# A graph layer with decaying weights: eight beats to a difference in three unmarked pairs, and their products four slots later

## The reference

```python
h = relu(layernorm(x))
support = h @ weight
mask = (adj != 0)
rank = cumsum(mask, axis=1)
deg = rank[:, -1:]
k = minimum(deg, 100)
pos = rank - (deg - k)
w = mask * where(pos > 0, 0.5 ** (k - pos), 0)
out = x + w @ support + bias
```

## Time and profile before

| what | us |
|---|---|
| median of 3 runs (216.24 to 216.45) | 216.44 |
| the profiled execution | 216.8 |
| its span in the trace | 214.2 |
| PE busy | 196.7 (92%) |
| DVE busy | 196.8 (92%) |
| ACT busy | 160.6 (75%) |

### The profile page before, as it was taken

The page is one execution under the profiler, slowest core; times in us unless marked ns, Lnnn a source line. Parts: engine busy times, 40 slices in busy tenths (PEclk is TensorE's granted clock), DMA queues, the critical chain, the costliest instruction groups (busy, mean ns, idle before and its releaser), DMA issues.

```text
span 214.2 us, 6505 instructions
## 1 busy us (share of the span) xinstructions
PE 196.7 (92%) x2784; PEld 188.0 (88%) x2784; DVE 196.8 (92%) x239; ACT 160.6 (75%) x303; POOL 29.1 (14%) x53
## 2 busy tenths in 40 slices
PE   0369979999999999999999999999999999999993
PEld 0269657997898999999999999999999999999993
DVE  1999979797979999999999999989999999998893
ACT  2442996786786988778778778789978989998720
POOL 7800000000010404010004110500000000000000
PEclk9999999999999999999999999999999999999999
DMA  6999999999999999999999999999998000000001
GB/s 203 204 217 220 216 211 216 216 219 212 218 213 221 210 218 216 213 220 216 211 222 212 217 218 215 216 217 218 221 209 174 8 12 3 12 15 3 17 0 43
DMA packets 7677, 36.09 MB, mean 168 GB/s; under 512 B 1506, under 2 KB 3298, under 8 KB 3554
## 3 DMA queue, kind: packets, MB, share of 16 engines
q0 software_dynamic: 4608, 33.56, 75.1%
q1 hardware_dynamic: 2882, 2.10, 3.8%
q10 hardware_dynamic: 160, 0.03, 0.1%
HBM read 68.19 MB, written 1.05 MB: 323 GB/s over the span
## 4 chain that ended last, share of the span: by engine, by line
PE 81%; DVE 7%; ACT 6%; DMA 2%; issue 1%; SPq 0%; DVEq 0%
PE acc L633 40%; PE chain L626 25%; PE chain L624 14%; ACT powers L313 3%; ACT support L296 3%; DMA x_sb<-in_x 2%; DVE masks L358 2%; PE chain L612 2%; DVE sq_sum L460 1%; DVE powers L455 1%; DVE later L399 1%; DVE row_sum L451 1%; DVE part L364 1%; DVE acc L481 0%; DVE sums L364 0%
## 5 line engine op out<-in xcount | busy, mean ns | idle before, releaser
L313 ACT ACTIVATE powers<-chain 128x512 int16<-128x512 f32 (+1 forms) x279 | 148.7, 573 | 33.6 <-PE chain L626 31.4
L633 PE MATMUL acc<-support,powers 128*128 128x192 bf16 x1024 | 159.5, 246 | 1.3 <-ACT powers L313 1.2
L626 PE MATMUL chain<-diag_own,masks 128*128 128x128 bf16 x608 | 107.1, 219 | 0.1
L624 PE MATMUL chain<-diag_past,masks 128*128 128x128 bf16 x568 | 102.2, 219 | 2.1 <-ACT powers L313 1.5
L633 PEld LDWEIGHTS acc<-support,powers 128*128 128x128 bf16 x1024 | 95.9, 98 | 4.3 <-ACT powers L313 2.4
L358 DVE TENSOR_SCALAR masks<-adj_b 128x4096 uint8<-128x4096 bf16 x32 | 72.6, 2281 | 5.0 <-DMA adj_b<-in_adj 5.0
L624 PEld LDWEIGHTS chain<-diag_past,masks 128*128 128x128 fp8e3 x568 | 55.5, 99 | 5.3 <-ACT powers L313 3.9
L626 PE MATMUL chain<-diag_step,masks 128*128 128x128 bf16 x416 | 60.1, 219 | 0.0
L626 PEld LDWEIGHTS chain<-diag_own,masks 128*128 128x128 fp8e3 x608 | 59.7, 99 | 0.3 <-issue 0.3
L626 PEld LDWEIGHTS chain<-diag_step,masks 128*128 128x128 fp8e3 x416 | 39.5, 99 | 0.0
L242 POOL DMA_DIRECT2D adj_b<-in_adj x32 | 24.5, 767 | 108.9 <-DVE masks L358 107.7
(11 more groups left out here) (52 smaller groups left out, 66.3 us busy)
## 6 DMA issues: line engine op xcount, KB each, us to landing
adj_b<-in_adj POOLq DMA_DIRECT2D x32, 1024.0 KB, 35.0
x_sb<-in_x SPq DMA_DIRECT2D x2, 512.0 KB, 4.5
out<-x_sb SPq DMA_DIRECT2D x14, 64.0 KB, 5.4
out<-x_sb SPq DMA_DIRECT2D x4, 32.0 KB, 9.5
w<-in_L_gnn_weight ACTq DMA_DIRECT2D x2, 16.0 KB, 9.1
bias<-in_L_gnn_bias SPq DMA_DIRECT2D x1, 0.2 KB
```

What stands on the lines that cost most here:

```text
L313: nc.scalar.activation(powers[:, c, b, cols].bitcast(i16), chain[c][:, cols], ACT.Relu, bias=(MAX_NEIGH + 1) * STEP).then_inc(powers_ready ...
L624: nc.tensor.matmul(chain[c][:, at:at + P], column(n, t + 1), diag_past[:, :], start=False, stop=False, skip_group_check=True)
L626: return nc.tensor.matmul(chain[c][:, at:at + P], column(n, t), diag_own[:, :] if marked else diag_step[:, :], start=False, stop=True, ski ...
L633: return nc.tensor.matmul(acc[u % ACCS][:, k * 3 * D:(k + 1) * 3 * D], powers[:, u % FLIGHT, s + 1 if k < MARKS[u] else s, at:at + P], sup ...
```

## The change

`BATCH` of units 8, 11 and 14 goes from 4 to 8, so that each has two floors and two differences instead of four: the first floor of 9 beats (4608 columns), the second of 8 (4096), differences of 8 beats (4096 columns). The first difference moves from slot STARTS + 5 to STARTS + 9, the second stays where the fourth was, at STARTS + 17. `LAGS` of units 8, 11, 14 and also 15 (whose batches stay at 4) grow by four. The other edits are new tables that are empty (`PAIRED`, `TWINS`), with branches for them that issue what was issued before, one PSUM tensor of four banks in place of four of one bank each, and another numbering of the eight load buffers.

```diff
-    LAGS = [8, 5, 9, 10, 9, 10, 9, 8, 9, 8, 10, 12, 11, 11, 11, 10, 9, 8]
-
-    BATCH = [4, 4, 4, 4, 4, 4, 4, 4, 4, 4, 4, 4, 4, 4, 4, 4, 4, 4]
+    LAGS = [8, 5, 9, 10, 9, 10, 9, 8, 13, 8, 10, 16, 11, 11, 15, 14, 9, 8]
+
+    BATCH = [4, 4, 4, 4, 4, 4, 4, 4, 8, 4, 4, 8, 4, 4, 8, 4, 4, 4]
...
+    PAIRED = ()
+
+    TWINS = ()
...
-        acc = [pb(f"acc{a}", [P, 512], fp32) for a in range(ACCS)]
+        accs = pb("accs", [P, ACCS, 512], fp32)
+        acc = [accs[:, a, :] for a in range(ACCS)]
...
-                pool.dma_start(adj_b[:, n % LOADS, :], adj_t[n]).then_inc(adj_loaded[n % LOADS], 16)
+                pool.dma_start(adj_b[:, (n + SHIFT) % LOADS, :], adj_t[n]).then_inc(adj_loaded[n % LOADS], 16)
...
-                    pe.wait_ge(rows_done[u % ACCS], u // ACCS)
+                    pe.wait_ge(rows_done[added_with(u - ACCS) % ACCS], sets_until(u - ACCS))
```

More of the change, by code:

```diff
@@ L92, in batches_until, with added_with, sets_until, units_of @@
         return sum(STEPS[v] // BATCH[v] for v in range(u % FLIGHT, u, FLIGHT) if MARKS[v] < SIZES[v])
+    def added_with(u):
+        return u - 1 if u - 1 in PAIRED else u
+    def sets_until(u):
+        f = added_with(u)
+        return sum(added_with(v) == v for v in range(f % ACCS, f + 1, ACCS))
+    def units_of(f):
+        return [f, f + 1] if f in PAIRED else [f]
     def halved_until(u):
         return sum(2 if CHAINS[v] == 2 else 1 for v in range(u))
+    SETS = [u for u in range(NU) if added_with(u) == u]
     SLOTS = max(STARTS[u] + LAGS[u] + STEPS[u] for u in range(NU))
@@ L206, in gnn_decay_kernel, with planes_of_both @@
         RUNS_OF = [CHAINS[UNIT_OF[n]] * P for n in range(NT)]
+        def planes_of_both(u):
+            at = (FIRST[u] + SHIFT) % RING
+            return masks[:, at:at + 2, :].rearrange("q k (r e) -> q (k r) e", e=2)\
+                .rearrange("q (j r) e -> q j r e", r=2 * CHAINS[u] * P)
         def planes_of(n):
-            return masks[:, (n + SHIFT) % RING, :].rearrange("q (j r e) -> q j r e", r=RUNS_OF[n], e=2)
+            u, at = UNIT_OF[n], (n + SHIFT) % RING
+            if u in TWINS:
+                both = planes_of_both(u)
+                k = n - FIRST[u]
+                return both[:, :, k * RUNS_OF[n]:(k + 1) * RUNS_OF[n], :]
+            return masks[:, at, :].rearrange("q (j r e) -> q j r e", r=RUNS_OF[n], e=2)
         def in_planes(tensor, n):
@@ L228, in _ @@
             sp.dma_start(bias_1[:, :], bias.rearrange("(a d) -> a d", a=1)).then_inc(bias_loaded, 16)
-            for u in range(NU):
-                sp.wait_ge(rows_done[u % ACCS], u // ACCS + 1)
-                rows = slice(FIRST[u], FIRST[u] + SIZES[u])
+            for u in SETS:
+                sp.wait_ge(rows_done[u % ACCS], sets_until(u))
+                rows = slice(FIRST[u], FIRST[u] + sum(SIZES[v] for v in units_of(u)))
                 sp.dma_start(out_t[:, rows, :], x_sb[:, rows, :]).then_inc(stored, 16)
-            sp.wait_ge(stored, 16 * NU)
+            sp.wait_ge(stored, 16 * len(SETS))
         @block.gpsimd
@@ L357, in mask, with mask_both @@
                     dve.wait_ge(chain_ready[u % FLIGHT], taken_until(u) + TAKEN[u])
[L358 removed]
+                nc.vector.tensor_scalar(planes_of(n), in_planes(adj_b[:, (n + SHIFT) % LOADS, :], n), 0.0, 1.0,
                                         ALU.not_equal, ALU.mult).then_inc(mask_ready, 1)
+            def mask_both(u):
+                n = FIRST[u]
+                for k in range(2):
+                    dve.wait_ge(adj_loaded[(n + k) % LOADS], 16 * ((n + k) // LOADS + 1))
+                if n >= RING:
+                    v = UNIT_OF[n + 1 - RING]
+                    dve.wait_ge(chain_ready[v % FLIGHT], taken_until(v) + TAKEN[v])
+                    v = UNIT_OF[n - RING]
+                    dve.wait_ge(chain_ready[v % FLIGHT], taken_until(v) + TAKEN[v])
+                at = (n + SHIFT) % LOADS
+                two = adj_b[:, at:at + 2, :].rearrange("q k (r e) -> q (k r) e", e=2)\
+                    .rearrange("q (r j) e -> q j r e", r=2 * RUNS_OF[n])
+                nc.vector.tensor_scalar(planes_of_both(u), two, 0.0, 1.0,
+                                        ALU.not_equal, ALU.mult).then_inc(mask_ready, 2)
             def halve(u, ins, outs, done):
@@ L532, in _ @@
                     to = STARTS[u] - LEADS[u] - g
-                    if u >= 3 and to == 8 and FIRST[u] > 3:
+                    if u >= 3 and to == 8 and FIRST[u] > 3 and u not in TWINS:
                         mask(FIRST[u])
                     if u >= 3 and to == 7 and SIZES[u] > 1:
-                        mask(FIRST[u] + 1)
+                        if u in TWINS:
+                            mask_both(u)
+                        else:
+                            mask(FIRST[u] + 1)
                     if u >= 3 and to == 6:
@@ L546, in _ @@
                         scan(u, 1)
-                    done = STARTS[u] + LAGS[u] + STEPS[u]
+                    if added_with(u) != u:
+                        continue
+                    done = max(STARTS[v] + LAGS[v] + STEPS[v] for v in units_of(u))
                     if g == done:
```

43 lines of the change are left out of this document (29 added, 14 removed).

## The result

The changed kernel takes 219.16 us (218.75 to 219.34, 4 runs), the one before 216.34 (215.96 to 216.45, 4 runs): a ratio of 1.0118 with a 95% interval of 1.0096 to 1.0141, 2.8 us more. The forecast was 218.8. The profiled execution is the slowest of the four, 219.34, with a span of 216.7 us against 214.2.

The account below looks back on a forecast made before the run. PE was taken as the bound from slot 36 on. The terms -1.25 + 1.32 - 0.77 + 0.58 - 0.64 + 2.64 + 0.29 made +2.17 on the profiled 216.8, 218.97, taken as 218.8 us; range 217.4 to 220.1.

Parts of the forecast that it names:

- The bound and its price: From slot 36 on PE is the bound; a product costs 0.082 us, a count 0.056; slots 107 to 114 get +2.64.
- Slots 54 to 57: They lose unit 8's products, 1.32 us; base 10 then waits for its scans, 0.06 with the pause, 0.52 without: -1.25.
- Slots 75 to 78: They lose unit 11's products, 1.32 us; chain 1's rounds then hold them, 6.12 against 6.89 before: -0.77.
- Base 15: Slot 85: unit 15's scans end at 166.40 on DVE, PE comes at 165.86 and goes at 166.44: +0.58 us.
- Slots 95 to 98: They lose unit 15's products, 1.32 us; ACT's 12 beats at 0.50 hold them, 6.00 against 6.64 before: -0.64.
- The end: After unit 15's last product, its additions and one of unit 17 come between: last addition starts 0.29 us later.
- The fixed part, and ACT's cycles: Skill's estimates: 58 cycles per DVE instruction, 0.7 us for twelve; 0.57 us per ACT beat, 220.0 in all.
- DVE's queue as the clock: Rival: DVE's queue sets the time and gets faster, 0.8 us less on DVE pulling the rest along: 215.6; 7%.
- ACT's pace of 0.553: Rival: slots 95 to 98 last as long as before (+0.64), slots 75 to 78 some 0.3 longer: 219.8; 15%.
- PE idling nowhere: Rival: beats and rounds overlap better, both stretches give back all 1.32: 216.6 to 217 at best; 7%.
- The step from 218.6 to 218.8: Median stands 0.36 below the profiled execution, giving 218.6; slot 56's pause, likely part of that, was already absorbed: 218.8.
- the pause of slot 56: PE pause without a releaser in the profile of before, 0.46 us, likely part of the profiled execution's 0.36 excess.

Follow-up runs that it names:

- the lags alone: Kernel before with the new LAGS and all batches at 4 beats (narrow, four-beat floors): 218.75 us, ratio 1.0098.
- The products-first run: Changed kernel, but in each group PE issues the four products first and waits for the beat only ahead of the counts: 218.66 us, ratio 1.0107.
- the runs with one unit: Kernel before with only unit 14 (LAG 15, BATCH 8) or only unit 15 (LAG 14) changed: 217.72 us and 217.30 us.

## Why the prediction was right, and where its steps were off

*The bound and its price.* Right. 100 products took 8.41 us at the end, (8.41 - 0.25) / 99 = 0.082 each, and the tail grew by 2.64 us. With unit 14 or unit 15 alone the tail grew by 1.32. What the products cost where they land was forecast to the hundredth; the rest is how much the earlier slots give back.

*Slots 54 to 57.* Right in mechanism: base 10 waited 0.32 for its scans here, 0.52 with unit 8 alone and 0.45 with the lags alone. I blamed the nine-beat floor for the fact that less work ahead of the scans didn't help; the run with four-beat floors has much the same wait, so the floor makes no difference that shows. The -1.25 holds against the trace with the pause; without the pause it is -0.78.

*Slots 75 to 78.* The mechanism is right, the size off: -0.51 for -0.77. The term that was mis-sized is the 0.06 us from a beat's end to the next group. I had read it off a group that begins with a count; chain 1's begins with a product. ACT and PEld in the changed kernel, the beat of unit 13 in slot 76 and the weight load that it releases:

```profile
150.93 0.60 ACT L341 ACTIVATE powers<-chain 128x512 int16<-128x512 f32 x1
...
151.64 0.10 PEld L698 LDWEIGHTS accs<-support,powers 128*128 128x128 bf16 x1 [0.25 <-ACT powers L341]
```

The load comes 0.11 after the end and the matmul at 151.67, 0.14 after it, so the round is 151.67 - 149.96 = 1.71, not 1.63. Three rounds of 0.08 more make 0.24 of the 0.26. The number was there to be read in the trace of before: fifteen product groups in slots 8 to 35 start 0.14 after the beat that they wait for, the one of slot 24 at 51.15. Which groups get the 0.14 is in the last section.

*Base 15.* The right place, and the length of the path on DVE within 0.1 us of the working. Its first and last row in the changed kernel:

```profile
142.99 1.36 DVE L469 TENSOR_SCALAR powers<-powers 128x4608 int16<-128x4608 int16 x1 [1.20 <-ACT powers L341]
...
165.36 1.28 DVE L453 TENSOR_TENSOR_SCAN later<-sums 128x257 bf16<-128x257 uint8 x2
```

From the floor at 142.99, 0.23 later than I had it, to the end of the scans at 166.64 are 23.65 us, for 23.64. The wait was 0.34 for 0.58: the scans came 0.24 later than forecast and PE 0.50 later, and the 0.26 between them is what slots 75 to 78 didn't give back. The run with narrow batches shows that the wait hangs on the wide ones. (The 0.13 us that I took for 512 more columns of a floor isn't in the rows that I named, which give 0.72 - 0.61 = 0.11; the floors of 4608 and 4096 columns cost the 1.28 and 1.13 from start to start that it gave.)

*Slots 95 to 98.* -0.54 for -0.64, but for a reason that I had put second, and so the nearness of the number is in part luck. ACT's own pace doesn't hold them: in a full queue it is 0.478, so 12 beats would be 5.7. It is chain 1's round (unit 16 with products of unit 13), 1.41 plus the same 0.08, 1.49 in the place of ACT's 1.50; its groups start 1.54, 1.49 and 1.53 apart, the 0.04 where its beat stands behind another one on ACT. That the two forecasts lay so near each other hid the error in both. The products-first run took the rounds away and showed what stands behind them, ACT's queue at base 17 and DVE's additions of unit 11, at 6.1 us again.

*The end.* The additions cost 0.07 for 0.29: this term was too large by 0.22, and that the row has +0.27 is chance.

*The fixed part, and ACT's cycles.* The Trainium skill's fixed part of a DVE instruction ("VectorE: DVE Perf Modes", section "The TRN2 errata"), 58 cycles at 0.96 GHz and so by estimate 0.06 us, is in the changed trace: 2.288 for a difference of 4096 against twice 1.222 of 2048 is 0.156 of busy time, of which about 0.09 is the overlap of neighbours in the rows and 0.066 the fixed part. The cycles that the same section of the Trainium skill has for ScalarE from PSUM, 172 and one per column at 1.2 GHz and so by estimate 0.57 us at 512 columns, are no pace here: queued beats start 0.478 apart, and the measurement decides.

*The rivals.* DVE's queue as the clock gave 215.6; with the new lags, wide batches are no faster than narrow ones (219.16 and 218.75), so less DVE work earned nothing. ACT's pace of 0.553 is excluded by the queued beats, PE idling nowhere by the runs with one unit. What no rival of mine said: in slots 95 to 99 three limits (rounds 6.05, ACT 5.7, additions 6.1) stand within a few tenths of each other, so that taking one away uncovers the next.

*By the sum*: +2.17 forecast for the trace, +2.54 measured (the sum of the table). Of these, +0.60, -0.35 and the 0.20 behind the last addition belong to the execution of the changed kernel or to that of before, and 0.46 of the -1.25 is the pause of before; without all four it is +2.55. The medians say +2.8, with an interval of 2.1 to 3.1 us (216.34 by 0.0096 and 0.0141), and that holds both this and the +2.4 of the forecast (218.8 from 216.44). The step from 218.6 to 218.8, which took the pause of slot 56 for one that most executions don't have, was right: five of the seven traces that leave unit 8's products in place are without it. The median of before that the forecast started from was 0.1 higher than the one beside it.

## What to carry to other kernels

When one engine is full from start to end, moving its work in time costs nothing only where it lands in slots that are limited by something else. Work that leaves a slot saves no more than the distance to that slot's next limit (here the round from PE over ACT back, and DVE's list), and work that reaches the tail, where nothing runs beside it, is paid in full. So for each place that loses work, write down the second limit with its length, and for each that gains, what runs beside it; here that gave the loss to about half a microsecond before anything was run. Twelve instructions saved on DVE, as busy by the page as PE, were worth nothing here, and one that is twice as long delays what is queued behind it: base 15 by 0.34 us, and with the old lags two products by 0.9 each.

## What the runs showed of the hardware that was not expected

Beats of ACT (128 x 512 from PSUM, float32 to int16) that find their input ready start 0.478 us apart, but the duration in their rows grows, by 11 to 14 ns each, from 592 to 717 in eleven beats of the changed kernel with products first. The starts stay 0.478 apart meanwhile, so in a full queue the row's duration isn't all work, and only the distance of starts is a pace.

A matmul that waits for ACT's beat starts 0.06 us after the beat's end when it is a count and 0.14 when it is a product. The product loads another type (bfloat16 powers, where the count loads fp8e3 masks), and ACT wrote what it loads, but the bases show that neither is the reason. A base loads bfloat16 that DVE wrote. In the traces of all twelve kernels the 52 bases that wait for DVE's scan start 0.06 after its end, and base 17 of the changed kernel with products first, which waits for a beat, starts 0.14 after it (188.05 and 188.19). What goes with the number is the place of the wait in PE's program. A count has one wait ahead of it. A base has the scan's first and the beat's second, a product that of its weights first and the beat's second. Where the only or the first wait is the last to be met, it is 0.06 in nearly all cases; where it is the second, 0.14 or 0.15 in 160 of 165 products. No run was made to test this, and why the second wait should cost more isn't shown.
